# One Trainium2 core, two kinds of attention in a chain of blocks: attention heads paired on the two halves of the array in pass 1, causal mask added inside the maximum

## The reference, cut to what matters

```python
def attention(x, ...):                    # 16 heads of 8 channels, rotary positions on q and k
    q, k, v = heads(x @ wq + bq), heads(x @ wk + bk), heads(x @ wv + bv)
    q, k = rope(q), rope(k)
    att = einsum('bhtd,bhsd->bhts', q, k) / sqrt(8)
    att = where(causal, att, -inf)
    y = einsum('bhts,bhsd->bhtd', softmax(att), v)
    return merge(y) @ wp + bp

def mixture(x, ...):                      # 8 heads of 64, 5 experts, 2 chosen per head and token
    scores = einsum('bhid,bhjd->bhij', q * scale, k)
    attn = einsum('bhij,bhjd->bihd', softmax(scores), v)
    return einsum('bthe,bthk,ekd->btd', mask_o, attn, Wo)

x = x + attention(layernorm(x), a...);  x = x + mixture(layernorm(x), ...)
x = x + attention(layernorm(x), b...);  x = x + mixture(layernorm(x), ...)
```

## Time and profile before

| | us |
|---|---|
| median of 3 runs | 2207.96 |
| lowest, highest | 2207.55, 2214.34 |
| profiled execution | 2209.6 |
| its span in the profile | 2207.9 |
| a steady iteration | 128.1 |

### The profile page before, as it was taken

The page is one execution under the profiler, slowest core; times in us unless marked ns, Lnnn a source line. Parts: engine busy times, 40 slices in busy tenths (PEclk is TensorE's granted clock), DMA queues, the critical chain, the costliest instruction groups (busy, mean ns, idle before and its releaser), DMA issues.

```text
span 2207.9 us, 40511 instructions
## 1 busy us (share of the span) xinstructions
PE 1899.7 (86%) x11328; PEld 913.1 (41%) x11328; DVE 1637.4 (74%) x2950; ACT 1275.3 (58%) x2803; POOL 1045.1 (47%) x1124
## 2 busy tenths in 40 slices
PE   1758998899898889989888998989899898998775
PEld 0323444435354443535444353544434354443433
DVE  4548787877878787787878777787877777796561
ACT  0326657575665757566575756657575665757452
POOL 1214455462635546263554626355462635555433
PEclk8779999999999999999999999999999999999977
DMA  3121212020121202012120201212020121200000
GB/s 95 42 34 30 34 40 35 28 34 17 34 34 40 34 28 35 16 35 33 40 34 28 36 16 36 31 40 34 28 37 21 34 28 39 34 6 13 10 10 5
DMA packets 87623, 68.19 MB, mean 31 GB/s; under 512 B 10720, under 2 KB 83104, under 8 KB 87328
## 3 DMA queue, kind: packets, MB, share of 16 engines
q1 hardware_dynamic: 87456, 66.62, 16.5%
HBM read 32.51 MB, written 10.49 MB: 19 GB/s over the span
## 4 chain that ended last, share of the span: by engine, by line
PE 49%; DVE 29%; issue 12%; ACT 5%; DMA 2%; POOL 1%; DVEq 1%; SPq 0%; ACTq 0%; POOLq 0%; PEldq 0%; PEld 0%
DVE nmaxA L878 6%; PE Y L488 6%; PE S1c L429 4%; DVE ztmp L999 4%; DVE nmaxF L883 4%; PE S1b L429 4%; PE S2a L453 4%; PE M L619 3%; PE S2b L453 3%; PE Y L479 3%; PE S1a L429 3%; DVE rotated L924 2%; PE M L539 2%; ACT Pq L713 2%; PE M L592 2%
## 5 line engine op out<-in xcount | busy, mean ns | idle before, releaser
L1117 POOL TENSOR_TENSOR Z<-Z,ztmp 128x1280 f32<-128x1280 f32 x112 | 324.8, 2900 | 374.7 <-DVE ztmp L999 373.5
L1084 POOL TENSOR_SCALAR_AFFINE_SELECT PT<-PT 128x256 f32<-128x256 f32 (+1 forms) x640 | 248.3, 400 | 395.8 <-ACT PT L698 393.1
L1108 POOL TENSOR_TENSOR Vf<-Vf,ztmp 128x512 f32<-128x512 f32 x256 | 352.5, 1377 | 139.9 <-DVE ztmp L973 134.8
L698 ACT ACTIVATE PT<-S2a 128x512 f32<-128x512 f32 x320 | 191.1, 597 | 152.7 <-PE S2a L447 124.4
L488 PE MATMUL Y<-PT,Vf 128*64 128x512 f32 x1024 | 274.8, 617 | 0.0
L429 PE MATMUL S1a<-Kf,Qf 64*128 64x512 f32 x352 | 216.6, 698 | 6.6 <-ACT Pq L713 4.6
L973 DVE TENSOR_TENSOR ztmp<-xv,wv_s 128x512 f32<-128x512 f32 x256 | 219.7, 858 | 2.8 <-POOL Z L1117 2.8
L429 PE MATMUL S1c<-Kf,Qf 64*128 64x512 f32 x352 | 209.2, 676 | 12.6 <-ACT Pq L713 11.2
L702 ACT ACTIVATE PT<-S2a 128x512 f32<-128x512 f32 x256 | 153.1, 598 | 89.8 <-PE S2a L453 89.6
L698 ACT ACTIVATE PT<-S2b 128x512 f32<-128x512 f32 x320 | 191.3, 598 | 14.1 <-PE S2b L447 13.2
L429 PE MATMUL S1b<-Kf,Qf 64*128 64x512 f32 x320 | 190.8, 678 | 6.5 <-ACT Pq L713 6.5
(11 more groups left out here) (109 smaller groups left out, 3931.5 us busy)
## 6 DMA issues: line engine op xcount, KB each, us to landing
Qs<-parts SPq DMA_DIRECT2D x96, 128.0 KB
Ks<-parts SPq DMA_DIRECT2D x96, 128.0 KB
tab_s<-in_tab SPq DMA_DIRECT2D x16, 512.0 KB, 4.3
xr<-out_x SPq DMA_DIRECT2D x32, 256.0 KB, 2.8
out_x<-res SPq DMA_DIRECT2D x32, 256.0 KB, 2.2
wa_s<-in_wa SPq DMA_DIRECT2D x16, 320.0 KB, 2.9
xl<-out_x SPq DMA_DIRECT2D x16, 256.0 KB, 2.8
out_x<-in_x SPq DMA_DIRECT2D x8, 256.0 KB, 4.7
```

The costliest lines, as they stand in the source:

```text
L698: nc.scalar.activation(PT[:, slot % 2, b, :], t[:, :], ACT.Exp, scale=SCALE_A).then_inc(exps_done.sem, 1)
L1084: last = nc.gpsimd.affine_select(out=v, in_=v, compare_op=ALU.is_ge, fill=0.0, base=0, pattern=pattern, channel_multiplier=-1)
L1108: nc.gpsimd.tensor_tensor(Vf[:, i, :, :], Vf[:, i, :, :], vtmp[:, n % VBUF, :, :], ALU.add).then_inc(v_acc.sem, 1)
L1117: nc.gpsimd.tensor_tensor(Z[:, :, :, :], Z[:, :, :, :], ztmp[:, hh % 2, :, :, :], ALU.add).then_inc(z_acc.sem, 1)
```

## The change

`ROWS_P1` becomes 48 and pass 2 has 50 rows. Even heads lie on partitions 0 to 49 of `Qs` and `Ks`, odd heads on 64 to 113, and these tiles have 8 head columns instead of 16. The channel order of the projections and of the rotary tables follows (even heads first). The scatter issues 24 DMAs of 64 source partitions each instead of 12 of 128. Rows with the maxima go to 48, 49 and to 112, 113.

Pass 1 issues the banks of an even and an odd head together, after the bank two back has been read, each bank with a signal of its own. The banks are reordered so that neighbours belong to an even and an odd head; the 256s of heads 0 and 2 share one bank and those of 1 and 3 another. The mask products of line 421 are gone. VectorE adds a mask row `maskw` (zeros, then the triangle) in an operation that also takes the maximum, one for each head and query tile, 16 a group instead of 14 reductions. The sums are written over the scores in PSUM. The negation moves into `split_maxima`. Pass 2 keeps its order of one bank at a time with its own wait; only rows and bank order change. At the start one memset is added, the one on rows of ones becomes two, and the cast of the mask is gone.

```diff
-    ROWS_P1 = 96
+    ROWS_P1 = NSP * DA
     ROWS_P2 = ROWS_P1 + 2
+    HALF = 64
...
-    for pair in range(GA // 2):
-        h0, h1 = 2 * pair, 2 * pair + 1
-        for h in (h0, h1):
-            BANKS_A1 += [[(h, 3, 0)], [(h, 2, 0), (h, 0, 384)]]
-            BANKS_A2 += [[(h, 0, 0)], [(h, 1, 0), (h, 3, 384)]]
-        BANKS_A1.append([(h0, 1, 0), (h1, 1, 256)])
-        BANKS_A2.append([(h0, 2, 0), (h1, 2, 256)])
+    for h0 in range(0, GA, 2):
+        BANKS_A1 += [[(h, 3, 0)] for h in (h0, h0 + 1)] + [[(h, 2, 0), (h, 0, 384)] for h in (h0, h0 + 1)]
+        BANKS_A2 += [[(h, 0, 0)] for h in (h0, h0 + 1)] + [[(h, 1, 0), (h, 3, 384)] for h in (h0, h0 + 1)]
+    BANKS_A1 += [[(h, 1, 0), (h + 2, 1, 256)] for h in (0, 1)]
+    BANKS_A2 += [[(h, 2, 0), (h + 2, 2, 256)] for h in (0, 1)]
...
-        Qs = sb("Qs", [ROWS_P2, HA, T], BF)
-        Ks = sb("Ks", [ROWS_P2, HA, T], BF)
+        Qs = sb("Qs", [P, HA // 2, T], BF)
+        Ks = sb("Ks", [P, HA // 2, T], BF)
...
                         for r in range(NSP):
-                            sp.dma_start(dst[DA * r:DA * r + DA, :, :],
-                                         parts[:, qk, order[r], :]).then_inc(scattered.sem, 16)
+                            for lo in (0, HALF):
+                                sp.dma_start(dst[lo + DA * r:lo + DA * r + DA, :, :],
+                                             parts[lo:lo + HALF, qk, order[r], :]).then_inc(scattered.sem, 16)
...
-                    if group >= SA and b % GF:
+                    if b % 2:
                         return
...
-                    pe.wait_ge(*s1_free(j, (n if group < SA else n + 1) - len(S1)))
+                    pe.wait_ge(*s1_free(j, n + 1 - len(S1)))
                     if group < SA:
-                        for h, qt, col in BANKS_A1[b]:
-                            hh, keys = GA * group + h, (qt + 1) * P
-                            nc.tensor.matmul(t[:, col:col + keys], Qs[0:ROWS_P1, hh, qt * P:keys],
-                                             Ks[0:ROWS_P1, hh, 0:keys], start=True, stop=False)
-                            last = nc.tensor.matmul(t[:, col + qt * P:col + keys], identb[:, :], maskb[:, :],
-                                                    start=False, stop=True)
-                        last.then_inc(s1_filled.sem, 1)
+                        for i in range(2):
+                            for h, qt, col in BANKS_A1[b + i]:
+                                hh, keys, r = GA * group + h, (qt + 1) * P, HALF * (h % 2)
+                                last = nc.tensor.matmul(S1[(n - 1 + i) % len(S1)][:, col:col + keys],
+                                                        Qs[r:r + ROWS_P1, hh // 2, qt * P:keys],
+                                                        Ks[r:r + ROWS_P1, hh // 2, 0:keys], start=True, stop=True)
+                            last.then_inc(s1_filled.sem, 1)
...
                         for h, kt, col in BANKS_A2[b]:
-                            hh = GA * slot + h
-                            last = nc.tensor.matmul(t[:, col:col + T - kt * P], Ks[0:ROWS_P2, hh, kt * P:kt * P + P],
-                                                    Qs[0:ROWS_P2, hh, kt * P:T], start=True, stop=True)
+                            hh, r = GA * slot + h, HALF * (h % 2)
+                            last = nc.tensor.matmul(t[:, col:col + T - kt * P],
+                                                    Ks[r:r + ROWS_P2, hh // 2, kt * P:kt * P + P],
+                                                    Qs[r:r + ROWS_P2, hh // 2, kt * P:T], start=True, stop=True)
...
+                        apart(dve)
+                        for h, qt, col in BANKS_A1[b]:
+                            keys = (qt + 1) * P
+                            last = nc.vector.tensor_tensor_reduce(
+                                t[:, col:col + keys], t[:, col:col + keys], maskw[:, T - keys:T], 1.0, -3.0e38,
+                                ALU.add, ALU.max, maxA[:, h % 2, GA // 2 * group + h // 2, qt:qt + 1])
                         last.then_inc(s1_read.sem, 1)
...
-                    nc.vector.tensor_copy(nmb[:, 0, :, :], src).then_inc(maxA_chain.sem, 1)
+                    nc.vector.tensor_scalar(nmb[:, :, 0, :, :], src, -1.0, None, ALU.mult).then_inc(maxA_chain.sem, 1)
...
-                    nc.vector.tensor_tensor(nmb[:, 1, :, :], src, nmb[:, 0, :, :], ALU.subtract).then_inc(nmb_ready.sem, 1)
+                    nc.vector.scalar_tensor_tensor(nmb[:, :, 1, :, :], src, -1.0, nmb[:, :, 0, :, :], ALU.mult,
+                                                   ALU.subtract).then_inc(nmb_ready.sem, 1)
```

More of the change, by code:

```diff
@@ L97, in attention_and_mixture @@
         identb = sb("identb", [P, P], BF)
[L98 removed]
+        maskw = sb("maskw", [P, T])
         wa_s = sb("wa_s", [P, 5, C])
@@ L205, in attention_and_mixture @@
         x_copied = Signal("x_copied", B, 16)
-        consts_cast = Signal("consts_cast", 2)
-        dve_init = Signal("dve_init", 6)
+        consts_cast = Signal("consts_cast", 1)
+        dve_init = Signal("dve_init", 8)
         xlA_loaded = Signal("xlA_loaded", 1, 16)
@@ L316, in rows @@
                     apart(sp)
-                    for i in range(2):
-                        sp.dma_start(Qs[ROWS_P1 + i:ROWS_P1 + i + 1, GA * group:GA * group + GA, :],
-                                     mrowA[i * GA * NT:(i + 1) * GA * NT, :]).then_inc(rowsA_in.sem, 16)
+                    for odd in range(2):
+                        r = HALF * odd + ROWS_P1
+                        sp.dma_start(Qs[r:r + 2, GA // 2 * group:GA // 2 * (group + 1), :],
+                                     mrowA[odd * GA * NT:(odd + 1) * GA * NT, :]).then_inc(rowsA_in.sem, 16)
                 if f_end:
@@ L683, in _ @@
             nc.scalar.activation(identb[:, :], ident[:, :], ACT.Copy).then_inc(consts_cast.sem, 1)
-            nc.scalar.activation(maskb[:, :], maskf, ACT.Copy).then_inc(consts_cast.sem, 1)
             def iteration(j, a, f, f_end, a_prep, f_prep):
@@ L815, in _ @@
             nc.vector.memset(minus_half[:, :], -0.5).then_inc(dve_init.sem, 1)
-            dve.wait_ge(dve_init.sem, 5)
-            nc.vector.memset(Ks[ROWS_P1:ROWS_P2, :, :], 1.0).then_inc(dve_init.sem, 1)
+            dve.wait_ge(dve_init.sem, 6)
+            for lo in (0, HALF):
+                nc.vector.memset(Ks[lo + 32:lo + HALF, :, :], 1.0).then_inc(dve_init.sem, 1)
             dve.wait_ge(dve_init.sem, dve_init.per)
@@ L869, in maxima @@
                     if group < SA:
-                        segs = BANKS_A1[b]
-                        h0, qt0, _ = segs[0]
-                        if len(segs) == 2 and segs[1][1] == qt0:
-                            last = nc.vector.tensor_reduce(nmaxA[:, GA * group + h0:GA * group + h0 + 2, qt0],
-                                                           t[:, :].rearrange("p (h k) -> p h k", h=2), AX.X, ALU.max,
-                                                           negate=True)
-                        else:
-                            for h, qt, col in segs:
-                                last = nc.vector.tensor_reduce(nmaxA[:, GA * group + h, qt:qt + 1],
-                                                               t[:, col:col + (qt + 1) * P], AX.X, ALU.max, negate=True)
+                        apart(dve)
[4 more added lines that the diff above has]
+                                ALU.add, ALU.max, maxA[:, h % 2, GA // 2 * group + h // 2, qt:qt + 1])
                         last.then_inc(s1_read.sem, 1)
@@ L1160 @@
     H, D = 16, C // 16
-    plain = [h * D + d for d in range(D) for h in range(H)]
-    swapped = [h * D + (d + D // 2) % D for d in range(D) for h in range(H)]
+    plain = [h * D + d for odd in range(2) for d in range(D) for h in range(odd, H, 2)]
+    swapped = [h * D + (d + D // 2) % D for odd in range(2) for d in range(D) for h in range(odd, H, 2)]
     def layout(wq, wk, wv, wp, bq, bk, bv, bp):
@@ L1184 @@
         cos, sin = np.cos(ang), np.sin(ang)
-        tabs.append(np.stack([np.repeat(np.concatenate([cos, cos]), H, 0), np.repeat(np.concatenate([-sin, sin]), H, 0)], 1))
+        rows = [np.tile(np.repeat(np.concatenate(t), H // 2, 0), (2, 1)) for t in ((cos, cos), (-sin, sin))]
+        tabs.append(np.stack(rows, 1))
     Wv, Wo = np.asarray(L0_ffn_Wv), np.asarray(L0_ffn_Wo)
```

16 lines of the change are left out of this document (8 added, 8 removed).

## The result

The changed kernel takes 2280.56 us (median of 4 runs, 2275.61 to 2285.02), the kernel before 2207.76 beside it: a ratio of 1.0325, with an interval from 1.0288 to 1.0362. It is slower, 22 us beyond the predicted 2259 and inside the predicted range. The sign and the main reason hold; but that the sum comes out near is in part luck: two errors of opposite sign in it, and a term of some 35 us that it lacked.

The account below looks back on a forecast made before the run. No single engine was the bound: VectorE paces 33 of pass 1's 40 banks, TensorE seven. 4.6 + 0.8 - 1.0 - 0.4 - 0.8 = +3.2 us an iteration, times 16 = +51, gave 2259 us; range 2175 to 2345.

Parts of the forecast that it names:

- Two instructions: VectorE, pass 1: each masked maximum is a main instruction plus a separate accumulator read, priced at 0.08 us.
- the read does not overlap: Rival, VectorE in pass 1: the accumulator read costs its full 0.20 us, +9.6 us an iteration, 2361 us; chance 0.13.
- the maximum costs nothing extra: Rival, VectorE in pass 1: the maximum comes with the main instruction, -1.8 us an iteration, 2179 us; chance 0.22.
- Its size: VectorE, pass 1: reads and merged banks add 1.40 us a group, the main part 0.015 us an instruction.
- What it falls on: Pass 1: VectorE's added time counts for 33 of 40 banks; seven hide in its 2.8 us idle in slot 6.
- The gains: Per iteration, credits of 1.0 us for waits, 0.4 in slot 6 and 0.8 in slots 2 and 3.
- Slot 6, 0.4 us: TensorE, pass 1: 0.55 us a group saved, counted for 0.7 of a group in slot 6: 0.4 us.
- Slots 2 and 3, 0.8 us: TensorE, pass 2: half-height tiling spares eight pairs the switch in front of them, 0.8 us an iteration.
- Waits, 1.0 us: VectorE: earlier filled banks, mainly the last of slot 7, and fewer mask-product gaps save 1.0 us an iteration.
- Pairs: TensorE, pass 1: pairs of 512 take 0.22 us, of 384+128 0.40, of 256s 0.33; tiling switches 0.10 each way.
- The clock: Rival, TensorE: one more 3.4 us stretch at 1.2 GHz an iteration, 27 us on top, 2286 us; chance 0.08.
- The scatter: SP: 24 half-size DMAs end 1.2 us later, inside some 4 us of slack, so no steady cost.

Follow-up runs that it names:

- a_pad8: The changed kernel with eight semaphore increments put ahead of VectorE's code, which only moves the loop's code; 2243 us.
- a_nomask: The changed kernel with the old reductions on VectorE, so the mask is left out of the maximum and the mask products stay gone; 2190.11 us, ratio 0.9903.
- a_pad40: The changed kernel with 40 semaphore increments put ahead of VectorE's code; 41 us above the kernel before.
- b_nomask: The kernel before without its mask products, so the mask is left out of the maximum; 2201.2 us, ratio 0.9975.
- b_pad26: The kernel before with 26 semaphore increments put ahead of VectorE's code and nothing of the change; 32 us above the kernel before.
- b_pad34: The kernel before with 34 semaphore increments put ahead of VectorE's code and nothing of the change; 13 us below the kernel before.

## Why the prediction was right, and where it was wrong

**Two instructions: right.** The profile has 1024 accumulator reads.

```profile
L878 DVE DVE_READ_ACCUMULATOR2_ANT maxA<- 128x1 f32 x1024 | 145.0, 142 | 0.0
```

The Trainium skill ("VectorE: DVE Perf Modes", section "Two Vector instructions with no wait between them") calls such an operation two instructions; the trace agrees, 16 a group. The rival "the read does not overlap" falls by the equal starts at 973.48. The rival "the maximum costs nothing extra" was nearer than I had it: the read itself takes no start of its own. It falls because the main part does cost, 0.02 to 0.08 us an instruction in these rows and mostly more than the 0.034 that it allowed, and by the 53 us of a_pad8 less a_nomask.

**Its size: too large.** I charged 1.40 us a group for the reads and the merged banks and 0.24 for the main part, 1.64 together. With the upper of the spacings the starts give 4 x 0.04 + 4 x 0.10 + 2 x 0.16 = 0.88, and VectorE's busy time agrees: 58 us more, which is 64 x 0.9, where I had named 90. I had taken ScalarE's spacing of 0.09 behind its read (rows 5) as the near row; VectorE's read takes no start of its own. What is left is dearer on short pieces (0.05 each on 384 and 128) than on 512. On the path it came to 53 to 59 us, where the sum had (4.6 + 0.8) x 16 = 86.

**What it falls on: right in slot 6, not elsewhere.** I let seven of 40 banks hide in VectorE's idle time in slot 6. The masked maximum costs 0.23 us there (a_pad8 18.45, a_nomask 18.22), which is what the three banks that don't hide should cost at the measured price, 3 x 0.09. In slots 7 and 0 it costs 1.4 and 1.9, where VectorE got only 0.9 more to do in each, and in slot 1 it costs 0.5. At the measured price my 33 banks would be 3.3 x 0.9 x 16 = 48 us; the runs have 53 to 59. Why slots 7 and 0 lose more than VectorE's own time isn't shown.

**The gains: too large.** I credited 1.0 + 0.4 + 0.8 = 2.2 us an iteration, 35 us; the runs show 18 (before less a_nomask). The term that was mis-sized is that of slots 2 and 3.
- *Slot 6, 0.4 us: 0.28 there.* The mask products gave 0.54 (18.50 to 17.96), near the 0.7 x 16 x 0.06 = 0.67 of the sum. Halves and pairs cost 0.26 (17.96 to 18.22), the sum's own 0.7 x (1.0 of switches - 0.63 of overlap); this agreement is luck, since the overlap is larger than I said (below). VectorE's 0.23 took the rest: the net is 18.45 against 18.50.
- *Slots 2 and 3, 0.8 us: not there.* Slot 2 gained 0.3 to 0.4 in every kernel with halves and pairs, but slot 3 went up by 0 to 1.0. Their sum is 34.0 to 35.1 us in these kernels against 34.35, and 35.1 in a_nomask, a loss of 0.7. Why slot 3 grows is open.
- *Waits, 1.0 us: there, and then used up.* The 0.80 us of idle time before the last bank (rows 3) are gone in a_nomask, and VectorE reaches the edge sooner. It shows behind the edge: slot 0 takes 10.92 us in a_nomask against 12.69 before (about 0.5 of it because the standstill is shorter, 24.1 us for twelve against 30.5). Slot 7 is 0.2 above before. With the masked maximum in, this gain and more is gone: slot 7 lost 1.8 us. The price is on TensorE: its waits for VectorE before pass 1 rise from 57 us to 120 in a_nomask and 171 after.

The last bank and the edge in a_nomask:

```profile
1045.61 0.68 DVE L879 TENSOR_REDUCE maxA<-S1c 128x2 f32<-128x512 f32 x1
1048.18 0.17 DVE L902 CAST nmb<-maxA 128x16 bf16<-128x16 f32 x1 [1.89 <-issue]
```

**Pairs: more overlap than I said, same price of the switch.** I had the inner two of 384, 128, 384, 128 overlap (0.40 us); they all do. The last product of the pair starts at 1071.28 and the transposes at 1071.43, 0.15 us for 128 columns that take 0.06, so 0.09 for the switch, and there are 0.53 us from the start of the four transposes at 1070.57 to the pair, where before the same four handed over in 0.44 (1041.89 to 1042.33). Pass 2 and pass 1 of unlike halves overlap too (1118.75 and 1118.77), which I had left out. None of it was worth much, since TensorE's time in pass 1 counts for less than half.

**The missing term: the place of the code.** The last of rows 2 showed VectorE doing nothing for 2.5 us, and I read it only as "the edge". I never asked what it would do if the program got longer. It is worth 32 to 37 us. So the working is: predicted 86 - 35 = +51; measured 54 - 18 = +36 for the change itself, and 37 for the second standstill, 73 together (differences along one chain of kernels, before, a_nomask, a_pad8, after, so they add up by construction; with a_pad40 in the place of a_pad8 they are 59 - 18 and 32). The predicted time was near because an oversized term stood in for one that I didn't have.

**The clock: underrated, its price open.** From the page, 2 x (1 - clock) x span is the time at 1.2 GHz: before 2 x 0.055 x 2208 = 243 us, after 2 x 0.099 x 2283 = 452. In slots 0 and 1 the mean granted clock is 0.69, where rows 2 have 0.91. In the iteration shown, TensorE falls to 1.2 GHz after the wait of 1.75 us at 973.67 (a pair of 512 takes 0.60 us, not 0.39), is back at 2.4 GHz by 990.58, and falls again after two more waits for VectorE, 1.76 and 2.62 us:

```profile
976.45 0.60 PE L422 MATMUL S1b<-Ks,Qs 48*128 48x512 bf16 x1 [0.46 <-DVE maxA L878]
...
990.58 0.39 PE L422 MATMUL S1c<-Ks,Qs 48*128 48x512 bf16 x1
...
993.82 0.33 PE L422 MATMUL S1b<-Ks,Qs 48*128 48x384 bf16 x1 [1.76 <-DVE maxA L878]
...
997.71 0.39 PE L422 MATMUL S1a<-Ks,Qs 48*128 48x256 bf16 x1 [2.62 <-DVE maxA L878]
```

(The last takes 0.39 us; 256 columns take 0.28 at 2.4 GHz.) My rival gave one more such stretch of 3.4 us an iteration; there are about 13 us (209 / 16). The slower VectorE is only a part of it. By the same sum the time at 1.2 GHz is 243 us before, 295 without the mask products (b_nomask), 355 with halves and pairs (a_nomask), 382 with the masked maximum (a_pad8) and 452 with the second standstill (after). The first two of these steps made the kernel faster, so time at 1.2 GHz is no price by itself. In the standstill there is a comparison: it adds 70 us at 1.2 GHz to the changed kernel (78 against a_pad40) but only 16 to the kernel before (b_pad26, 259), and costs 37 (32) and 32 us. So the clock can hardly be more than a few us of it; as the kernels differ otherwise too, I call that likely and not shown.

**The scatter: hidden, the sign of its term wrong.** SP's issues after:

```profile
1034.15 7.91 SPq L364 DMA_DIRECT2D Qs<-parts  x12
1046.36 8.04 SPq L364 DMA_DIRECT2D Ks<-parts  x12
```

The 24 small transfers end near 1057.6 and pass 1 first reads them at 1066.86, so 9 us of cover are left. They took not 1.2 us more but less: 10.5 us for each 12 (1034.9 to 1045.4 and 1047.1 to 1057.6), 21 together, where before twelve of double the size took 25 (993.1 to 1018.3). No wait on the scatter stands in the steady part, as predicted. The packets' share of the 16 DMA engines over the whole run says the same, 13.9% against 16.5% for the same 66.62 MB. The one-off parts didn't quite cancel: the wait for the scatter in the first two iterations fell from 40.4 to 34.4 us, but the first residual of the mixture (line 1011 before) is added 5 us later in a_pad8 than before (328.3 against 322.8).

## What to carry to other kernels

Price a new instruction from starts, on the shapes that it will have, and don't borrow the spacing of another engine; then price a gain only where that engine ends the wait, and subtract the wait that the same edit tightens. Look at what an engine does at the loop's back edge ("issue" before its first instruction): it depends on the length of the code ahead of it, so compare two versions with the standstills equal, by putting a few do-nothing instructions ahead of the loop, before you say what an edit costs. And ask whether a step is needed at all: here the mask in the maximum wasn't, and leaving it out beat both kernels.

## What the runs showed of the hardware

- VectorE stands still for 1.9 to 2.7 us each time that the loop goes back, once, twice or not at all, depending on how many instructions stand ahead; 8 to 34 increments moved the time by 13 to 45 us of 2200 (b_pad26 to b_pad34 is 45). Where it didn't stand still, 60 fewer packets of instructions were fetched.
- VectorE's accumulator read is shown with 142 ns, but the next operation starts with it: up to 0.04 us more than a plain reduction on 512 columns, 0.05 on 384 or 128, 0.08 on 256.
- Products on rows 0 to 49 and 64 to 113 run side by side whole, and across program order: the second bank's 384 (1071.11) starts ahead of the first bank's 128 (1071.28), which was issued before it. The Trainium skill ("TensorE: Matmul & The Clock Gate", section "The mechanism" in the part on packing small matmuls) says that products keep the program's order in start and end; these rows differ, and the measurement decides. Signals on the last product of each bank are right all the same, since each half keeps its own order in these rows.
- The same bytes took less time as 24 DMAs of 64 KB than as 12 of 128 KB: 21 us against 25.
